# Typed message rows of 26 of 49 node blocks made during the in-degree count

## The chip, the cores and the metric

One core of a Trainium2 chip runs one program. The metric is the device time of one execution in microseconds (us), lower is better. Engines are named as in the profile: PE (TensorE, matrix products and transposes), PEld (its weight loads), DVE (VectorE), ACT (ScalarE), POOL (GpSimd) and SP (SyncE, which only issues DMAs). SPq is the instruction stream of SP.

## The reference, cut to what matters

Four graph layers run over 6250 nodes and 206250 edges, each followed by a residual and a layer norm. The change touches only the first layer. With `W_e` (3 edge types) and `W_n` (3 node types) it computes

```
src = node_feature[edge_src]
parts = [relu(node_feature)]
for t in range(3):
    msg = where(edge_type == t, relu(src @ W_e[t].T + b_e[t]), 0)
    parts.append(segment_sum(msg, edge_dst))
agg = concatenate(parts, axis=1)
updated = where(node_type == t, agg @ W_n[t].T + b_n[t], ...)
```

The kernel multiplies before it sums: for each node and each of the 9 pairs (edge type, node type) it makes one row of 128 numbers, `relu(x W_e[t]) W_n[k]`. Edges gather these **typed rows** later by source, edge type and target's type. So the table of typed rows, `typed_msgs` (49 blocks of 128 nodes, 1152 float32 numbers each, 576 KB per block), must be complete in memory before the gathers begin.

## The kernel before, in words

The program is a sequence of blocks; all engines meet at the end of each. Three of them matter here.

**First block (to about 240 us).** SP loads the edge arrays and then issues, on its one DMA queue and in this order: small paddings (L399 to L403), the copy of all edge features from the input to an internal table (L404, 51.6 MB), seven stores that blank `marks` (L409), and a tail store of `edge_pairs` (L410), and waits for the paddings. Meanwhile the in-degrees are counted. The count has `HB` = 101 steps. In each, DVE makes two sets of one-hot columns (`hist_hot`, L358 and L359) in one of two buffers, and PE adds 16 products of them to a sum (`hist_sum`, L366). `hist_hot` of step n waits until PE has finished step n-2 (`s_hist_mm`), `hist_sum` until its own columns are there (`s_hist_hot`). PE has its steps in a loop of `TB` = 4. After the count, DVE works out edge places and makes the fields of each edge, with small products of PE in between. ACT has nothing to do in this block after it has moved the transposed weights at about 31 us.

**Second block.** SP stores the edge fields; DVE works on a bias.

**Third block, the slot tables (about 266 to 626 us).** 44 steps of a second count (`outs(0, AHEAD)`), and then `GB` = 62 steps n, each of which makes one table of slots: DVE and ACT pick columns, PE transposes them (L1212), ACT and DVE store the result, SP sends it out (`slot_tabs`, L1001), and a share of the other 57 steps of the second count is done. Beside each of the first 49 steps the typed rows of a block pass through the engines, one stage per step: `turn` (PE, L1186, transposes the block of `X` into `ps[2]`), `turned` (ACT, L1150), `message` (PE, L1192, three products into `ps[3]`; ACT, L1156, three relus), `rows` (PE, L1199, three products 384 wide into `ps[4]`, `ps[6]`, `ps[7]`; ACT, L1163 and L1164, copies them to `zrows[b % 2]`), and SP stores `zrows` to `typed_msgs` (L990). Each stage has its semaphore: `s_xT`, `s_xTe`, `s_m`, `s_me`, `s_z`, `s_ze`. There are `MZ` = 2 buffers `zrows`, so the copies of block b wait until the store of block b-2 has landed (`s_mst`). PE's `rows(b)` waits for `s_ze` of block b-1, since it writes the same banks. At step 12 SP loads `marks` back, at step 20 DVE fills them forward, and at step 23 SP stores `edge_pairs`.

The queues and the order within each engine are written out by hand; nothing is planned or reordered by a scheduler.

Of the kernel before, what the change touches and what calls it, by code (L numbers as in the profile page):

```python
# [24 lines left out]
P = 128  # L25
N, E, D, T, FE = 6250, 206250, 128, 3, 64
NB = -(-N // P)
# [120 lines left out]
def build(nc, x, src, dst, attr, etype, weight, ntype, w_e, b_e, w_n, b_n, w1, b1, w3, w3e, b3, out):  # L148
    ctx = ExitStack()
    with ctx:  # L150
# [224 lines left out]
        def along_t(v, n):  # L375
            return v.rearrange("p (g t) -> p g t", t=TU).unsqueeze(2).to_broadcast([P, TG, n, TU])

        in_count = ps[5][:, 0:NB]
        out_count = ps[5][:, 64:64 + NB]

        with nc.Block() as block:
            @block.sync
            def _(sp):

                for col, a in ((src_i, src), (dst_i, dst), (typ_i, etype), (w_c, weight)):
                    sp.dma_start(col[:, 0:EC], a[0:MAIN].rearrange("(p c) -> p c", p=P)).then_inc(s_edges, 16)

                sp.dma_start(next_i[:, 0:EC], dst[1:MAIN + 1].rearrange("(p c) -> p c", p=P)).then_inc(s_edges, 16)
                sp.wait_ge(s_filler, 7)

                for col, a in ((dst_i, dst), (src_i, src), (typ_i, etype), (w_c, weight)):
                    sp.dma_start(col[0:EREST, EC:C], a[MAIN:E].rearrange("(p c) -> p c", c=1)).then_inc(s_rest, 16)
                sp.dma_start(next_i[0:EREST - 1, EC:C], dst[MAIN + 1:E].rearrange("(p c) -> p c", c=1)).then_inc(s_rest, 16)
                sp.dma_start(ntype_i[:, 0:NFULL], ntype[0:NFULL * P].rearrange("(b p) -> p b", p=P)).then_inc(s_rest, 16)
                sp.dma_start(ntype_i[0:NREST, NFULL:NB], ntype[NFULL * P:N].rearrange("(p c) -> p c", c=1)).then_inc(s_rest, 16)

                sp.wait_ge(s_fillf, 13)

                sp.dma_start(edge_fields[0:FRONT, :], front).then_inc(s_pads, 16)  # L399
                tail = slice(FRONT + E, FRONT + E + FILL)  # L400
                sp.dma_start(edge_fields[tail, :].rearrange("(p u) r -> p (u r)", u=U), fillf).then_inc(s_pads, 16)
                sp.dma_start(edge_feats[tail, :].rearrange("(p u) r -> p (u r)", u=U), fille).then_inc(s_pads, 16)
                sp.dma_start(by_place[E:BROWS, :], fillf[0:BROWS - E, 0:NF]).then_inc(s_pads, 16)  # L403
                sp.dma_start(edge_feats[FRONT:FRONT + E, :], attr).then_inc(s_feats, 16)  # L404
                spots = marks.rearrange("(p c) o -> p (c o)", p=P)
                width = MARKS // P
                for c0 in range(0, width, U * FE):
                    c1 = min(c0 + U * FE, width)
                    sp.dma_start(spots[:, c0:c1], fille[:, 0:c1 - c0]).then_inc(s_pads, 16)  # L409
                sp.dma_start(edge_pairs[FRONT + MARKS:EROWS, :].rearrange("(p c) r -> p (c r)", p=TAILP), tail_pairs).then_inc(s_pads, 16)  # L410
                sp.wait_ge(s_pads, 16 * (5 + -(-width // (U * FE))))


# [25 lines left out]
            def _(act):  # L439
# [19 lines left out]
                act.wait_ge(s_wT, T + T * (T + 1) + 2)  # L459
                act.copy(w3ew[:, :], ps[6][0:FE, 0:D]).then_inc(s_wTe, 1)  # L460
                act.wait_ge(s_x, 32)

            @block.tensor
            def _(pe):
# [12 lines left out]
                pe.wait_ge(s_wTe, T + 4)  # L477


                def ins(i, more=TB):  # L480
                    for j in range(more):
                        hist_sum(pe, in_count, i * TB + j, j % 2, opens=isinstance(i, int) and i + j == 0,
                                 closes=isinstance(i, int) and i * TB + j == HB - 1)
                in_steps(pe, PAIRS, ins)
                ins(PAIRS, DST_REST)

                pe.wait_ge(s_tot, 1)
                pe.matmul(ps[2][:, 0:NB], before[:, :], indeg, start=True, stop=True).then_inc(s_pref, 1)
                pe.matmul(ps[2][:, 64:64 + NB], ones[:, :], indeg, start=True, stop=True).then_inc(s_pref, 1)
                pe.wait_ge(s_end, 1)  # L490
                pe.transpose(ps[4][0:NB, 0:P], ends, ident).then_inc(s_endT, 1)
                pe.transpose(ps[4][0:NB, P:2 * P], steps_, ident).then_inc(s_endT, 1)
                pe.wait_ge(s_past, 1)
# [480 lines left out]
        with nc.Block() as block:  # L974
            @block.sync
            def _(sp):
# [7 lines left out]
                sp.dma_start(same_row[:, 0:CHUNKS].rearrange("o (p j) -> (o p) j", j=JB), same[0:CP, :]).then_inc(s_same_st, 16)  # L984
                sp.dma_start(same_row[:, CHUNKS:OVR], zeros[0:1, :]).then_inc(s_same_st, 16)
                for n in range(GB):
                    if 3 <= n < NB + 3:
                        b = n - 3
                        sp.wait_ge(s_ze, 2 * b + 2)
                        sp.dma_start(typed_msgs[b * P:(b + 1) * P, :], zrows[b % MZ]).then_inc(s_mst[b % MZ], 16)  # L990
                    if n == MARK_LOAD:
# [139 lines left out]
            @block.scalar  # L1131
            def _(act):
                def pick(n):
                    k = n % 2
                    here = slots_of(n)
                    slots_here(act, n)
                    at_least(act, s_slot_T, n - 1)
                    act.copy(sl_st[:, k * SLOTS:(k + 1) * SLOTS], here[:, :, SLOC])
                    act.copy(w_st[:, k * SLOTS:(k + 1) * SLOTS], here[:, :, WGT]).then_inc(s_slw_st, 1)

                def store(n):
                    k = n % 2
                    act.wait_ge(s_slot_T, n + 1)
                    at_least(act, s_slot_st[k], 16 * (n // 2))
                    act.copy(tabs[:, k, 0:3, :], ps[k][:, 0:3 * SLOTS].rearrange("p (r g) -> p r g", r=3)).then_inc(s_slot_e, 1)

                def turned(b):
                    act.wait_ge(s_xT, b + 1)
                    at_least(act, s_m, b - 1)
                    act.copy(xTs[b % 2], ps[2][:, 0:P]).then_inc(s_xTe, 1)  # L1150

                def message(b):
                    act.wait_ge(s_m, b + 1)
                    at_least(act, s_z, b - 1)
                    for t in range(T):
                        made = act.activation(mTs[b % 2][:, t * P:(t + 1) * P], ps[3][:, t * P:(t + 1) * P], ACT.Relu,  # L1156
                                              bias=beT[:, t:t + 1])
                    made.then_inc(s_me, 1)

                def rows(b):  # L1160
                    act.wait_ge(s_z, b + 1)
                    at_least(act, s_mst[b % MZ], 16 * (b // MZ))
                    act.copy(zrows[b % MZ][:, 0:T * D], ps[4][:, 0:T * D]).then_inc(s_ze, 1)  # L1163
                    act.copy(zrows[b % MZ][:, T * D:KINDS * D].rearrange("p (k c) -> p k c", k=2),  # L1164
                             psum[:, 6 * 512:8 * 512].rearrange("p (k c) -> p k c", k=2)[:, :, 0:T * D]).then_inc(s_ze, 1)

                for n in range(GB + 1):
                    if n < GB:
                        pick(n)
                    if n >= 1:  # L1170
                        store(n - 1)
                        if n - 1 < NB:
                            turned(n - 1)
                    if 2 <= n < NB + 2:
                        message(n - 2)
                    if 3 <= n < NB + 3:
                        rows(n - 3)

            @block.tensor
            def _(pe):  # L1180
                def outs(j0, j1):
                    for j in range(j0, j1):
                        hist_sum(pe, out_count, HB + j, (HB + j) % 2, opens=j == 0, closes=j == HB - 1)
                def turn(b):
                    at_least(pe, s_xTe, b)
                    pe.transpose(ps[2][:, 0:P], X[:, b * D:(b + 1) * D], ident).then_inc(s_xT, 1)  # L1186

                def message(b):
                    pe.wait_ge(s_xTe, b + 1)
                    at_least(pe, s_me, b)  # L1190
                    for t in range(T):
                        made = pe.matmul(ps[3][:, t * P:(t + 1) * P], weT[:, t * D:(t + 1) * D], xTs[b % 2], start=True, stop=True)  # L1192
                    made.then_inc(s_m, 1)

                def rows(b):
                    pe.wait_ge(s_me, b + 1)
                    at_least(pe, s_ze, 2 * b)
                    for t, to in enumerate((ps[4], ps[6], ps[7])):
                        made = pe.matmul(to[:, 0:T * D], mTs[b % 2][:, t * P:(t + 1) * P], wnT[:, (t + 1) * T * D:(t + 2) * T * D],  # L1199
                                         start=True, stop=True)  # L1200
                    made.then_inc(s_z, 1)

                outs(0, AHEAD)
                for n in range(GB):
                    k = n % 2
                    if n < NB:
                        turn(n)
                    pe.wait_ge(s_sb_st, n + 1)
                    pe.wait_ge(s_slw_st, n + 1)
                    at_least(pe, s_slot_w, n - 1)  # L1210
                    for r, st in enumerate((sl_st, sb_st, w_st)):
                        last = pe.transpose(ps[k][:, r * SLOTS:(r + 1) * SLOTS], st[:, k * SLOTS:(k + 1) * SLOTS], ident)  # L1212
                    last.then_inc(s_slot_T, 1)
                    if 1 <= n < NB + 1:
                        message(n - 1)
                    if 2 <= n < NB + 2:
                        rows(n - 2)
                    outs(*shares[n])


# [1098 lines left out]
```

## Time and profile before

| what | us |
|---|---|
| median of 3 runs | 5259.34 |
| lowest, highest run | 5254.54, 5260.63 |
| the profiled execution | 5261.47 |
| its span | 5259.7 |

The span is the time in which engines work; 1.8 us lie around it. The page's shares of busy time are means over the whole span, and say little about one block: PE is busy for 72% of the span, DVE for 62%, ACT for 23%. The change is read from the first 630 us. A row of a view of instructions gives the start, the duration of a group of neighbours (x16 is sixteen of them) and, in brackets, how long the engine had been idle and what ended that.

### The profile page before, as it was taken

Reading aid. Unit: us, or ns where it says so; the run is one execution under the profiler, and the core shown is the slowest. Engines: PE = TensorE matmul, PEld = TensorE weight load, DVE = VectorE, ACT = ScalarE, POOL = GpSimd, SP = SyncE. Lnnn points to the kernel's source line nnn. Section 1 sums busy time; section 2 is a strip of 40 time slices with the busy share of each in tenths; the row PEclk is TensorE's granted clock in tenths of the full one; section 3 lists DMA queues with packets and bytes.
Section 4 is the critical chain, followed back from the end, with each engine's and each line's share of the span. In section 5 each row is a group of like instructions: output and inputs, shape, how many; then the busy total and the mean of one; then the engine's idle time right before and its main releaser. Section 6 shows DMA issues by size and latency. Waiting matters only on the chain. (4 is left out here: it accounts for less than half of the span.)

```text
span 5259.7 us, 100150 instructions
## 1 busy us (share of the span) xinstructions
PE 3770.5 (72%) x38930; PEld 2751.6 (52%) x38930; DVE 3260.5 (62%) x4529; ACT 1204.4 (23%) x2110; POOL 2254.5 (43%) x2050
## 2 busy tenths in 40 slices
PE   4357755555555555377777676389999599989997
PEld 3345555555555555366666666345555244444444
DVE  7796898999999999455555554756666600230012
ACT  0025655555555555100000000400000200010000
POOL 0051378777777777577777777000000003000300
PEclk9998898999999999688998988699999799989998
DMA  9646797999999999865666656198888267656654
GB/s 315 212 115 238 236 343 276 327 346 340 336 338 340 343 344 330 222 165 166 171 165 165 169 162 158 22 332 305 301 305 304 91 203 227 198 165 202 217 187 142
DMA packets 695303, 1252.28 MB, mean 238 GB/s; under 512 B 366488, under 2 KB 511532, under 8 KB 685772
## 3 DMA queue, kind: packets, MB, share of 16 engines
q1 hardware_dynamic: 564028, 779.03, 46.1%
q10 hardware_dynamic: 60300, 314.88, 15.4%
q0 software_dynamic: 70576, 152.66, 11.4%
q8 instruction: 298, 4.88, 0.4%
q14 instruction: 101, 0.83, 0.0%
HBM read 792.49 MB, written 506.62 MB: 247 GB/s over the span
## 5 line engine op out<-in xcount | busy, mean ns | idle before, releaser
L1398 POOL DMA_INDIRECT big<-typed_msgs,big x988 | 1198.1, 1213 | 376.9 <-issue 307.8
L1446 PE MATMUL psum<-big 128*128 128x98 bf16 x7936 | 859.4, 208 | 649.8 <-DVE big L1428 629.4
L1446 PEld LDWEIGHTS psum<-big 128*128 128x128 bf16 x7936 | 766.0, 97 | 694.1 <-DVE big L1428 673.6
L2088 PE MATMUL psum<-big 128*128 128x512 bf16 (+1 forms) x4704 | 992.1, 373 | 82.6 <-DMA big<-adj 82.6
L1673 PE MATMUL psum<-big 128*128 128x192 f32 x3648 | 743.1, 364 | 307.8 <-DMA big<-typed_msgs,big 302.9
L1581 POOL DMA_INDIRECT big<-typed_msgs,big x836 | 830.8, 994 | 275.3 <-issue 244.8
L1673 PEld LDWEIGHTS psum<-big 128*128 128x128 f32 x3648 | 686.9, 215 | 371.8 <-issue 248.5
L1447 PE MATMUL psum<-big 128*128 128x49 bf16 x7936 | 845.5, 190 | 0.9 <-issue 0.9
L1448 PE MATMUL psum<-big 128*128 128x49 bf16 x7936 | 842.4, 186 | 2.7 <-issue 2.7
L1448 PEld LDWEIGHTS psum<-big 128*128 128x128 bf16 x7936 | 791.7, 100 | 3.1 <-issue 3.1
L2088 PEld LDWEIGHTS psum<-big 128*128 128x128 bf16 x4704 | 460.4, 98 | 605.9 <-DMA big<-adj 83.0
L1447 PEld LDWEIGHTS psum<-big 128*128 128x128 bf16 x7936 | 770.5, 97 | 11.1 <-issue 10.9
L1898 PE MATMUL psum<-big 128*128 128x416 f32 x1984 | 656.1, 494 | 63.4 <-DVE big L1932 62.4
L2135 POOL DMA_INDIRECT big<-spill,spill_row x98 | 92.7, 946 | 1420.0 <-DMA spill<-big 1390.7
L1428 DVE TENSOR_TENSOR big<-big 128x2400 bf16<-128x2400 bf16 x496 | 692.7, 1397 | 0.0
L1595 DVE SCALAR_TENSOR_TENSOR big<-iota,node,big 128x512 f32<-128x512 f32 x456 | 342.0, 750 | 517.4 <-PE psum L1673 502.5
L1425 DVE TENSOR_TENSOR big<-big 128x2048 bf16<-128x2048 bf16 x496 | 602.2, 1214 | 0.0
L1932 DVE STREAM_TRANSPOSE big<-big 128x3136 f32<-128x3136 f32 x124 | 427.2, 3445 | 239.6 <-PE psum L1898 221.2
L1486 ACT CAST big<-psum 128x784 bf16<-128x784 f32 x496 | 404.9, 816 | 675.7 <-PE psum L1448 574.7
L1898 PEld LDWEIGHTS psum<-big 128*128 128x128 f32 x1984 | 378.0, 191 | 341.1 <-issue 82.5
L1488 ACT COPY big<-psum 128x784 f32<-128x784 f32 x496 | 433.3, 874 | 0.0
L1423 DVE TENSOR_TENSOR big<-big 128x800 bf16<-128x800 bf16 x496 | 280.6, 566 | 68.9 <-POOLq L1402 50.1
(320 smaller groups left out, 2732.9 us busy)
## 6 DMA issues: line engine op xcount, KB each, us to landing
wadj<-big ACTq DMA_DIRECT2D x248, 784.0 KB
big<-wadj SPq DMA_DIRECT2D x124, 1568.0 KB, 7.3
big<-adj SPq DMA_DIRECT2D x210, 896.0 KB, 4.8
adj<-big ACTq DMA_DIRECT2D x62, 1568.0 KB
big<-staged SPq DMA_DIRECT2D x247, 384.0 KB, 3.3
staged<-big SPq DMA_DIRECT2D x61, 1536.0 KB
big<-edge_feats SPq DMA_DIRECT2D x456, 128.0 KB, 3.0
edge_feats<-in_edge_attr SPq DMA_DIRECT2D x1, 51562.5 KB, 163.3
```

The source lines that it names most:

```text
L1398: pool.indirect_dma_start(out=sgot4[:, c, u, 0:D], out_offset=None, in_=typed_rows, in_offset=bass.IndirectOffsetOnAxis(ap=pairs4i[:, g, u ...
L1425: dve.tensor_tensor(lo_b[:, q, :, :].rearrange("p t (c d) -> p t c d", d=2), in_twos(lo_ramp).to_broadcast([P, TT, P // 2, 2]), all_column ...
L1428: dve.tensor_tensor(hi_b[:, q, :, 1:4, :].rearrange("p t s (c d) -> p t s c d", d=2), hi.unsqueeze(2).to_broadcast([P, TT, 3, HC // 2, 2]) ...
L1446: pe.matmul(to[:, 0:2 * NB], lo, hi_b[:, q, t, 0:2, 0:NB], start=True, stop=False)
L1447: pe.matmul(to[:, NB:2 * NB], lo, hi_b[:, q, t, 2, 0:NB], start=False, stop=False)
L1448: last = pe.matmul(to[:, NB:2 * NB], lo, hi_b[:, q, t, 3, 0:NB], start=False, stop=True)
L1488: act.copy(wadj_st[:, k, b // 2, :, b % 2 * TT:(b % 2 + 1) * TT], made_in(b % 2)[:, :, NB:2 * NB].rearrange("p t s -> p s t")).then_inc(s_ ...
L1581: pool.indirect_dma_start(out=got4[:, h, u, 0:D], out_offset=None, in_=typed_rows, in_offset=bass.IndirectOffsetOnAxis(ap=pairs4i[:, g, u, ...
L1673: last = pe.matmul(ps[h][:, 0:ACCW], hot4[:, k, u, :], got4[:, pos % QG, u, :], start=(u == 0), stop=(u == U - 1))
L1898: last = pe.matmul(ps[c][:, 0:(b1 - b0) * 32], rows, turned[:, n % RT, q * QROW + b0 * 32:q * QROW + b1 * 32], start=(m == 0), stop=(m == ...
L1932: dve.transpose(turned[:, n % RT, :].rearrange("p (h i) -> p h i", i=32), wring[:, n % RW, :].rearrange("p (h g) -> p h g", g=32)).then_in ...
L2088: last = pe.matmul(ps[c % 2][:, 0:len(blocks) * P], terms_[:, k, b * D:(b + 1) * D], ring_a[:, m % RA, 0:len(blocks), s * P:(s + 1) * P], ...
```

## The change

`EARLY` = 26. The helpers of the typed rows move out of the third block, and are used in two places.

In the first block SP gets the stores of blocks 0 to 25 behind all that it issued before, ACT gets their work behind its last copy of weights, and PE's loop is written out, with the stages of a block between the steps of the count:

```
 # SP, behind L410
+for b in range(EARLY):
+    sp.wait_ge(s_ze, 2 * b + 2)
+    sp.dma_start(typed_msgs[b * P:(b + 1) * P, :], zrows[b % MZ]).then_inc(s_mst[b % MZ], 16)
 # ACT, behind wait_ge(s_x, 32)
+for j in range(EARLY + 2):
+    if j < EARLY:
+        turned(act, j, 0)
+    if 1 <= j < EARLY + 1:
+        relus(act, j - 1, 0)
+    if j >= 2:
+        rows_out(act, j - 2)
 # PE
-in_steps(pe, PAIRS, ins)
-ins(PAIRS, DST_REST)
+pe.wait_ge(s_x, 32)
+done = 0
+for n in range(HB):
+    hist_sum(pe, in_count, n, n % 2, opens=n == 0, closes=n == HB - 1)
+    while done < (n + 1) * (EARLY + 2) // HB:
+        if done < EARLY:
+            turn_x(pe, done, 0)
+        if 1 <= done < EARLY + 1:
+            messages(pe, done - 1, 0)
+        if done >= 2:
+            typed_out(pe, done - 2)
+        done += 1
 ...
 pe.wait_ge(s_end, 1)
+pe.wait_ge(s_ze, 2 * EARLY)
```

The new functions are the old ones; the two waits that matter are these:

```
+def rows_out(act, b):
+    act.wait_ge(s_z, b + 1)
+    at_least(act, s_mst[b % MZ], 16 * (b // MZ))
+    act.copy(zrows[b % MZ][:, 0:T * D], ps[4][:, 0:T * D]).then_inc(s_ze, 1)
 ...
+def typed_out(pe, b):
+    pe.wait_ge(s_me, b + 1)
+    at_least(pe, s_ze, 2 * b)
```

In the third block the 23 remaining blocks 26 to 48 take the places of the first 23 of the 49, so that its steps from n = 26 on have no typed work:

```
 for n in range(GB):
-    if 3 <= n < NB + 3:
-        b = n - 3
+    b = EARLY + n - 3
+    if EARLY <= b < NB:
         sp.wait_ge(s_ze, 2 * b + 2)
```

and likewise on ACT and PE, with b = EARLY + n in place of n.

## Rows read from the trace of the kernel before

**Rows 1.** Windows: stretch, its length, busy us of each engine, clock, DMA share, GB/s
```profile
34.35:159.25 124.90, 69.29 (x1164) 58.94 (x1165) 124.80 (x151) 0.00 (x0) 0.00 (x0) 1.00 1.00 332
...
506.49:591.20 84.71, 83.13 (x666) 63.38 (x665) 66.95 (x151) 69.05 (x193) 20.56 (x23) 1.00 0.95 329
594.84:624.30 29.46, 16.54 (x175) 11.65 (x172) 27.66 (x67) 10.06 (x26) 5.92 (x6) 0.55 0.57 185
```
**Rows 2.** Groups by line, 40.86 to 203.72 us: busy us, mean ns, idle before, releaser
```profile
L358 DVE TENSOR_TENSOR big<-ramp,big 128x2048 bf16<-128x2048 bf16 x101 | 122.8, 1216 | 0.0
L366 PE MATMUL psum<-big 128*128 128x49 bf16 x1600 | 95.5, 229 | 77.1 <-DVE big L359 77.1
```
**Rows 3.** Instructions in order of time, the count's start, DVE's 25th step, its end
```profile
40.86 1.23 DVE L358 TENSOR_TENSOR big<-ramp,big 128x2048 bf16<-128x2048 bf16 x1
...
42.70 0.94 PE L366 MATMUL psum<-big 128*128 128x49 bf16 x16 [12.05 <-DVE big L359]
...
45.70 1.22 DVE L358 TENSOR_TENSOR big<-ramp,big 128x2048 bf16<-128x2048 bf16 x1
...
79.56 1.22 DVE L358 TENSOR_TENSOR big<-ramp,big 128x2048 bf16<-128x2048 bf16 x1
...
203.72 1.68 DVE L585 CAST big<-big 128x1612 f32<-128x1612 int32 x1
...
225.88 0.21 DVE L605 COPY degs<-psum 128x49 f32<-128x49 f32 x1 [0.15 <-DVE small L601]
```
**Rows 4.** Issues of SP in the first block, in order of time
```profile
34.35 0.68 SPq L404 DMA_DIRECT2D edge_feats<-in_edge_attr  x1
35.08 124.13 SPq L409 DMA_DIRECT2D marks<-big  x7
159.25 17.83 SPq L410 DMA_DIRECT2D edge_pairs<-big  x1
```
**Rows 5.** DMA issues of the page: KB each, median us from issue to landing
```profile
edge_feats<-in_edge_attr SPq DMA_DIRECT2D x1, 51562.5 KB, 163.3
```
**Rows 6.** Waits of SP, 0 to 240 us
```profile
SPq L381 <- DMA edge_pairs<-big: 23.5, 1, 23.5
```
**Rows 7.** The tile typed_msgs: its stores' issue, and all its DMAs' landing
```profile
L990 SPq DMA_DIRECT2D typed_msgs<-big x49: 319/326/3624, 367.4 to 592.7; - x49
...
DMA to landing us min/median/max: 2.8/4.9/24.7
```
**Rows 8.** PE in order of time, one step with typed work, clock at 1.00
```profile
499.90 0.31 PE L1186 MATMUL psum<-wide_ident,X 128*128 128x128 f32 x1
500.04 0.49 PE L1212 MATMUL psum<-wide_ident,big 128*128 128x128 f32 x3
500.37 0.83 PE L1192 MATMUL psum<-big,weT 128*128 128x128 f32 x6
501.04 2.10 PE L1199 MATMUL psum<-wnT,big 128*128 128x384 f32 x6
...
506.83 0.96 PE L366 MATMUL psum<-big 128*128 128x49 bf16 x16
507.61 0.31 PE L1186 MATMUL psum<-wide_ident,X 128*128 128x128 f32 x1
```
**Rows 9.** The same, after a gap of 17 us in PE's work
```profile
493.12 0.48 PE L1186 MATMUL psum<-wide_ident,X 128*128 128x128 f32 x1 [17.13 <-ACT big L1150]
493.39 0.85 PE L1212 MATMUL psum<-wide_ident,big 128*128 128x128 f32 x3
494.03 1.59 PE L1192 MATMUL psum<-big,weT 128*128 128x128 f32 x6
495.42 3.87 PE L1199 MATMUL psum<-wnT,big 128*128 128x384 f32 x6
499.12 0.95 PE L366 MATMUL psum<-big 128*128 128x49 bf16 x16
```
**Rows 10.** Windows, as rows 1: a gap in the slot tables
```profile
480.00:495.00 15.00, 1.88 (x9) 1.75 (x10) 1.96 (x6) 2.58 (x8) 0.00 (x0) 0.50 0.27 108
```
**Rows 11.** ACT's copies of typed rows, in order of time
```profile
545.24 0.48 ACT L1163 COPY big<-psum 128x384 f32<-128x384 f32 x1 [0.38 <-PE psum L1199]
545.61 0.81 ACT L1164 COPY big<-psum 128x768 f32<-128x768 f32 x1
```

More of the change, by code:

```diff
@@ L376, in along_t, with turned, relus, turn_x @@
             return v.rearrange("p (g t) -> p g t", t=TU).unsqueeze(2).to_broadcast([P, TG, n, TU])
+        EARLY = 26
+        def turned(act, b, b0):
+            act.wait_ge(s_xT, b + 1)
+            if b >= b0 + 2:
+                act.wait_ge(s_m, b - 1)
+            act.copy(xTs[b % 2], ps[2][:, 0:P]).then_inc(s_xTe, 1)
+        def relus(act, b, b0):
+            act.wait_ge(s_m, b + 1)
+            if b >= b0 + 2:
+                act.wait_ge(s_z, b - 1)
+            for t in range(T):
+                made = act.activation(mTs[b % 2][:, t * P:(t + 1) * P], ps[3][:, t * P:(t + 1) * P], ACT.Relu,
+                                      bias=beT[:, t:t + 1])
+            made.then_inc(s_me, 1)
+        def rows_out(act, b):
+            act.wait_ge(s_z, b + 1)
+            at_least(act, s_mst[b % MZ], 16 * (b // MZ))
+            act.copy(zrows[b % MZ][:, 0:T * D], ps[4][:, 0:T * D]).then_inc(s_ze, 1)
+            act.copy(zrows[b % MZ][:, T * D:KINDS * D].rearrange("p (k c) -> p k c", k=2),
+                     psum[:, 6 * 512:8 * 512].rearrange("p (k c) -> p k c", k=2)[:, :, 0:T * D]).then_inc(s_ze, 1)
+        def turn_x(pe, b, b0):
+            if b > b0:
+                pe.wait_ge(s_xTe, b)
+            pe.transpose(ps[2][:, 0:P], X[:, b * D:(b + 1) * D], ident).then_inc(s_xT, 1)
+        def messages(pe, b, b0):
+            pe.wait_ge(s_xTe, b + 1)
+            if b > b0:
+                pe.wait_ge(s_me, b)
+            for t in range(T):
+                made = pe.matmul(ps[3][:, t * P:(t + 1) * P], weT[:, t * D:(t + 1) * D], xTs[b % 2], start=True, stop=True)
+            made.then_inc(s_m, 1)
+        def typed_out(pe, b):
+            pe.wait_ge(s_me, b + 1)
+            at_least(pe, s_ze, 2 * b)
+            for t, to in enumerate((ps[4], ps[6], ps[7])):
+                made = pe.matmul(to[:, 0:T * D], mTs[b % 2][:, t * P:(t + 1) * P], wnT[:, (t + 1) * T * D:(t + 2) * T * D],
+                                 start=True, stop=True)
+            made.then_inc(s_z, 1)
         in_count = ps[5][:, 0:NB]
@@ L477, in _ @@
                 pe.wait_ge(s_wTe, T + 4)
[L480 to L483, printed above, removed]
-                in_steps(pe, PAIRS, ins)
-                ins(PAIRS, DST_REST)
+                pe.wait_ge(s_x, 32)
[10 more added lines that the diff above has]
+                        done += 1
                 pe.wait_ge(s_tot, 1)
@@ L1145, in store @@
                     act.copy(tabs[:, k, 0:3, :], ps[k][:, 0:3 * SLOTS].rearrange("p (r g) -> p r g", r=3)).then_inc(s_slot_e, 1)
[L1147 to L1165, printed above, removed]
                 for n in range(GB + 1):
@@ L1171, in _ @@
                         store(n - 1)
[L1172 to L1177, printed above, removed]
+                    b = EARLY + n
+                    if EARLY <= b - 1 < NB:
+                        turned(act, b - 1, EARLY)
+                    if EARLY <= b - 2 < NB:
+                        relus(act, b - 2, EARLY)
+                    if EARLY <= b - 3 < NB:
+                        rows_out(act, b - 3)
             @block.tensor
@@ L1183, in outs @@
                         hist_sum(pe, out_count, HB + j, (HB + j) % 2, opens=j == 0, closes=j == HB - 1)
[L1184 to L1201, printed above, removed]
                 outs(0, AHEAD)
@@ L1205, in _ @@
                     k = n % 2
-                    if n < NB:
-                        turn(n)
+                    b = EARLY + n
+                    if b < NB:
+                        turn_x(pe, b, EARLY)
                     pe.wait_ge(s_sb_st, n + 1)
@@ L1213, in _ @@
                     last.then_inc(s_slot_T, 1)
[L1214 to L1217, printed above, removed]
+                    if EARLY <= b - 1 < NB:
+                        messages(pe, b - 1, EARLY)
+                    if EARLY <= b - 2 < NB:
+                        typed_out(pe, b - 2)
                     outs(*shares[n])
```

## The prediction

> **What bounds the kernel now.** I read by stages, since the page's shares are means over blocks with different limits. First the windows: in the stretch of the in-degree count DVE is busy for 124.80 of 124.90 us and PE for 69.29, ACT for none, and the DMA engines are full at 332 GB/s; in the steady steps of the slot tables PE is busy for 83.13 of 84.71 us; in the table steps without typed work DVE is, for 27.66 of 29.46, and PE for only 16.54 [rows 1]. So DVE sets the pace of the count, PE that of a table step with typed rows, DVE that of one without. Then the groups of the count: DVE never waits, PE is idle for 77.1 us, always for DVE's columns [rows 2]. That idle time is where the change puts work. Last I read SP's own stream and its waits, because the change hangs 26 stores on it. There the reader is to see something that DVE's rows don't show. SP issues the feature copy at 34.35; its next seven small stores take 124.13 us to issue, and the one behind them 17.83 [rows 4]. The copy lands 163.3 us after its issue, at 197.7 [rows 5], and the last small store at 159.25 + 17.83 + 23.5 = 200.6, although it is tiny [rows 4, 6]. What SP issues behind the copy is held until the copy is through.
>
> **The change, part by part.** Times are those of the profiled execution.
>
> *(a) The stores of blocks 0 and 1.* SP is free for them only at 177.1, and they stand in the same queue behind a store that lands at 200.6 [rows 4, 6]. One of them is 576 KB: at the 332 GB/s of the copy [rows 1] 1.8 us. So the store of block 0 lands at about 200.6 + 1.8 = 202.4; the floor is 200.6 itself, the ceiling 200.6 + 4.9, the median landing of such DMAs [rows 7].
>
> *(b) Who waits for it.* There are two buffers, so ACT's `rows_out(2)` waits for that landing. PE's `typed_out(3)` waits for `rows_out(2)`. PE comes to it in the pass done = 5, which follows the first n with (n + 1) * 28 // 101 = 6, that is n = 21. Behind this wait stand all further `hist_sum`s of PE. DVE can still make columns 22 and 23, but those of step 24 need sum 22. In the kernel before they start at 79.56 [rows 3]. Now: landing 202.4, ACT's two copies 1.2 (545.24 to 546.42) [rows 11], PE's three wide products 2.1 [rows 8], sum 22 0.95: 206.6. The count is held by 206.6 - 79.6 = **127.0 us**. The stalls of the bursts before that vanish in it. Nothing in the program covers it: DVE has work at every moment of the count [rows 1], and all that it does behind it, up to the end of the block, comes later by as much; the other engines wait for DVE there. Bounds: 125 to 131, from the landing's.
>
> *(c) The bursts after that.* Each pass is a transpose, three products and three wide ones. At the high clock that is 0.14 + 0.67 + 1.94 = 2.75 us, by the starts 499.90, 500.04 (the slot's own transposes, left out), 500.37, 501.04 and the end of the wide ones at 502.98 (501.04 + 2.10, less the 0.16 that one group overlaps the next) [rows 8]. Let PE start sum n at S. The burst follows at S + 0.78 (506.83 to 507.61), sum n+1 ends at S + 0.78 + 2.75 + 0.95, and DVE can start columns n+3 0.04 later, at S + 4.52. In the kernel before it starts them at S + 3.00 (42.70 and 45.70) [rows 3, 8]. So a burst costs 1.5 us of DVE's time, though PE has the idle time on average: 77.1 us against 26 * 2.75 = 71.5; the two buffers can't spread it. At the low clock the burst is 0.27 + 1.39 + 3.70 = 5.36 [rows 9], and it costs 4.1. The passes 6 to 26 still hold DVE: 21. The ends are 21 * 1.5 = 32 and 21 * 4.1 = 86. After the long wait PE begins at the low level: a gap of 15 us has a granted clock of 0.50 (1.2 GHz), and the burst behind it runs slowly until about 499.7, six us into its work [rows 9, 10]. Then PE would be busy for 3.6 * 0.95 + 2.75 = 6.2 us of each 7.3; the steady table steps, busy nearly throughout, have 1.00 (2.4 GHz) and those at 56% have 0.55 [rows 1]. I take 2.0 a burst, nearer to the high clock: **42 us**.
>
> The Trainium skill (TensorE: Matmul & The Clock Gate, HAM oscillation) says that short bursts of products with waits between them can fall back to the low clock before each burst. By it the bursts would all be of the slow kind; the row of the gap agrees for a long pause, and no row shows one of 4 us between such bursts. This is the second rival below.
>
> *(d) ACT's work in the count.* It is idle there, and a table step, which holds the same work and that of the slots, takes it 69.05 / 22 = 3.1 us [rows 1], against 7 us from pass to pass; each piece is wanted one pass later. Nothing, and if ACT were late it would add its delay to a burst. The stores behind the hold: one every 7 us, landing in 3 to 5 [rows 7]; nothing.
>
> *(e) PE's loop written out.* The same instructions, more code to fetch, beside full DMA queues until 200 us but inside the hold; the third block's PE code is written out already, and a sum takes as long there, 0.96 us, as in the loop, 0.94 [rows 3, 8]. Nothing; up to 5 us if fetches come late.
>
> *(f) The wait for `s_ze` before PE's two transposes.* The last pass follows the last sum, and DVE works for 22.2 us after the count before it reads it (203.72 to 225.88) [rows 3]. Nothing.
>
> *(g) The slot tables.* 26 steps lose their typed work. A step with it takes 84.71 / 22 = 3.85 us, one without 29.46 / 10 = 2.95 [rows 1]: 26 * 0.90 = **23.4 us** gained. The rows without typed work ran at a clock of 0.55, so a slower PE is in them. Gaps at the load of `marks`, the fill and the store of `edge_pairs` (steps 12, 20, 23) are DMA or DVE and stay. Ends: 0 if the landings of the tables set the step anyway, 30 if the gaps shrink as 15 MB of stores leave this queue. I take what the rows give.
>
> **Sum.** 127.0 + 42 - 23.4 = +145.6, on the profiled 5261.5: 5407. The median of the runs is 2.1 us lower, so I forecast **5405 us**, 2.8% slower. Its own range is 5388 to 5430.
>
> **Rivals.** *Low clock in the bursts.* Same hold, 86 in place of 42: +189.6, 5449 by the median. For it: the clock is low when PE resumes, and each pass is followed by 4 us of thin work. Against: such a PE would be busy for 3.6 * 0.95 + 5.36 = 8.8 of each 9.9 us, and that is what raised it in the rows [rows 1, 9]. Range 5430 to 5480.
>
> *The stores get through.* Their data travel beside the copy and land in a few us. Then no hold; 25 bursts at 2.0 make +50, less 23.4: +27, 5286. Against it: the tiny store that landed at 200.6, and that a table store or typed store behind others took up to 24.7 us to land [rows 6, 7]; and SP comes to them only at 177.1, so this needs SP's issues to be faster too.
> The Trainium skill (DMA: Bandwidth & Descriptors, Queues, rings and completion order) says that data of one queue carry no barrier, so that a later one may finish before an earlier one. By that the stores could overtake the copy's last packets, 1 to 3 us, not the 120; the trace gives no sign of an overtaking.
>
> *The idle time of PE takes it all* (the other side). Place: the count. If the store of block 0 landed before PE reaches pass 5 at about 77 us, and DVE's columns were far enough ahead that 71.5 us of bursts fill the 77.1 us of idle time [rows 2], the count would keep its length and only the 23.4 be left: 5236. It decides only when both hold; the buffer count speaks against the second, rows 4 against the first.
>
> *No gain in the tables.* The landings of the slot tables set the step: +169, 5428.
>
> **How the numbers follow.** The forecast's case 0.66, low clock 0.20, stores get through 0.08, no gain 0.02, PE's idle time takes it all 0.04. The range of 8 in 10 takes the first two and the last but one, less their tails: 5380 to 5465. About 0.2% (10.5 us) is what a measurement can tell from no change. Slower 0.95, same 0.01, faster 0.04.
>
> **What would show it.** In the changed kernel's profile: DVE idle for some 120 us in the count from about 80 us on, released by PE, PE by ACT, ACT by a DMA of typed_msgs; the first store issued at about 197 with SP's issue stream full until then; the count's end at about 373 instead of 203.7; DVE waits of 1.5 (or 4) us behind each later pass with the clock to match; 36 table steps at 2.95. I am wrong if the first typed store is issued, and lands, before 177, if the count has no gap over 20 us, or if the second block begins before 380.

## The result and the profile after

The changed kernel takes 5423.86 us (median of 4 runs, 5419.55 to 5426.19) against 5259.99 (median of 4, 5254.54 to 5265.01): ratio 1.031, 95% interval 1.0294 to 1.0326. It is slower by 164 us; the profiled spans are 5422.8 and 5259.7, 163.1 apart. The forecast was 5405, range 5380 to 5465.

SP's issues in the first block of the changed kernel, in order of time; they answer to [rows 4]:

```profile
34.92 0.68 SPq L455 DMA_DIRECT2D edge_feats<-in_edge_attr  x1
35.64 123.85 SPq L460 DMA_DIRECT2D marks<-big  x7
159.53 18.09 SPq L461 DMA_DIRECT2D edge_pairs<-big  x1
177.66 216.02 SPq L464 DMA_DIRECT2D typed_msgs<-big  x26
```

The waits of all engines up to 420 us (us in total, times, longest):

```profile
DVE big L358 <- PE psum L366: 182.4, 26, 119.4
...
ACT big L401 <- DMA typed_msgs<-big: 121.3, 1, 121.3
PE psum L425 <- ACT big L402: 114.9, 1, 114.9
```

This is the hold, and its order is read from the right: a DMA, ACT, PE, DVE, one wait of each. The instructions at its end, in order of time:

```profile
201.49 0.48 ACT L401 COPY big<-psum 128x384 f32<-128x384 f32 x1 [121.27 <-DMA typed_msgs<-big]
201.87 0.80 ACT L402 COPY big<-psum 128x768 f32<-128x768 f32 x1
...
202.81 4.18 PE L425 MATMUL psum<-wnT,big 128*128 128x384 f32 x6 [114.93 <-ACT big L402]
...
206.79 1.76 PE L366 MATMUL psum<-big 128*128 128x49 bf16 x32
...
207.92 1.22 DVE L358 TENSOR_TENSOR big<-ramp,big 128x2048 bf16<-128x2048 bf16 x1 [119.39 <-PE psum L366]
...
217.45 1.22 DVE L358 TENSOR_TENSOR big<-ramp,big 128x2048 bf16<-128x2048 bf16 x1 [2.99 <-PE psum L366]
...
223.85 1.23 DVE L358 TENSOR_TENSOR big<-ramp,big 128x2048 bf16<-128x2048 bf16 x1 [1.47 <-PE psum L366]
```

DVE's 25th step starts at 207.92, not at 79.56 [rows 3]. The two rows of DVE after it are the waits for the first two bursts behind the hold. Three bursts of PE, by their wide products: the first, in which the clock rose, the second, at the high clock, and a later one at the low clock throughout:

```profile
213.60 2.89 PE L425 MATMUL psum<-wnT,big 128*128 128x384 f32 x6
...
220.80 2.10 PE L425 MATMUL psum<-wnT,big 128*128 128x384 f32 x6
...
311.01 3.67 PE L425 MATMUL psum<-wnT,big 128*128 128x384 f32 x6
```

The windows, with the columns of [rows 1]: the hold, the rest of the count, the slot tables; then the slot tables of the kernel before:

```profile
80.00:205.00 125.00, 8.95 (x64) 6.31 (x64) 5.39 (x7) 2.36 (x7) 0.00 (x0) 0.51 0.96 324
205.00:389.02 184.02, 151.17 (x1524) 118.21 (x1522) 126.05 (x155) 50.03 (x127) 0.00 (x0) 0.82 0.17 69
546.01:791.07 245.06, 159.41 (x1388) 118.34 (x1387) 187.52 (x425) 114.49 (x316) 55.90 (x52) 0.69 0.65 213
```

```profile
360.73:626.54 265.81, 213.73 (x1726) 162.41 (x1725) 193.16 (x425) 168.10 (x472) 51.49 (x52) 0.88 0.73 254
```

In the hold the DMA engines are full and PE, DVE and ACT nearly idle; behind it the DMA engines are nearly empty (0.17) and PE and DVE wait for each other.

The account, from the two traces: the count starts 0.6 us later (41.42 for 40.86); the hold is 207.92 - 79.56 - 0.6 = 127.8 (DVE's long wait of 119.4, 8.0 us of four waits for bursts before it, and small change); from there to the end of the count, at 389.02, it takes 181.1 us, before 203.72 - 79.56 = 124.2 [rows 3], so 56.9 more; the slot tables take 20.8 less. 0.6 + 127.8 + 56.9 - 20.8 = 164.5; the remaining 1.4 us come back later.

### The profile page after: what moved, and what is told of

It is laid out like the page before. It is cut to its first block and busy times, and to the rows that moved or that the text cites. A ratio compares the mean times of both kernels' runs of the same rounds, so it can differ in the third digit from the quotient of the medians.

```text
span 5422.8 us, 100007 instructions
## 1 busy us (share of the span) xinstructions
PE 3806.8 (70%) x38930; PEld 2770.6 (51%) x38930; DVE 3257.1 (60%) x4529; ACT 1213.1 (22%) x2110; POOL 2251.6 (42%) x2050
## 5 line engine op out<-in xcount | busy, mean ns | idle before, releaser
L358 DVE TENSOR_TENSOR big<-ramp,big 128x2048 bf16<-128x2048 bf16 x202 | 246.4, 1220 | 189.5 <-PE psum L366 189.4
```

## The experiments

All are edits of the changed kernel; the code shown for e4, e6 and e9 is against e2, e1 and e5. Ratios are to the kernel before on the same chip.

**e2: no stores in the count.** The 26 stores come from X (wrong contents) behind the last sum; ACT's `rows_out` waits for no landing of the first 26 blocks.

```
-for b in range(EARLY):
-    sp.wait_ge(s_ze, 2 * b + 2)
-    sp.dma_start(typed_msgs[b * P:(b + 1) * P, :], zrows[b % MZ]).then_inc(s_mst[b % MZ], 16)
 sp.wait_ge(s_pads, ...)
+sp.wait_ge(s_hist_mm, HB)
+for b in range(EARLY):
+    sp.dma_start(typed_msgs[b * P:(b + 1) * P, :], X[:, 0:KINDS * D]).then_inc(s_pads, 16)
```

> The changed kernel without SP's 26 stores in the count, so that nothing there waits for a landing; in their place 26 stores of the same size, from X (wrong contents), are issued behind the last sum of the count, and nothing in the block waits for them. Theory (the landing of the first store holds the count for 128 us, and 25 bursts cost 2.6 us each): the hold goes, 5260 + 65 - 21 = 5304 us, up to 5312 if the late stores delay the edge fields. Rival (PE and ACT can't keep up with the work in the count, whatever the stores do): the long wait stays, 5424. Second rival (most bursts cost nothing without the low clock of the long pause): 5275.

Measured: 5315.84, ratio 1.0099 (1.0073 to 1.0125). The long wait is gone; PE and ACT do all of the work without it. What is left is the bursts' cost, in DVE's waits up to 400 us:

```profile
DVE big L358 <- PE psum L366: 75.4, 26, 3.8
```

That is 2.9 us for each of 26; I had 2.6. The longest is near the 4.1 that the prediction works out for a burst at the low clock. The count takes 41.96 to 282.51, 240.6 us, 77.7 more than before.

**e3: the tables alone.** Blocks 0 to 25 are not made at all (their stores as in e2), PE's count has no typed work.

> The kernel before in the count (PE's steps written out, no typed work), and the changed one in the slot tables: blocks 0 to 25 are not made at all; as in e2, 26 stores from X are issued behind the count to keep the bytes. This prices the gain in the tables alone. Theory: 26 steps at 0.8 to 0.9 us, 5260 - 21 = 5239 us. Rival (the landing of the tables sets the step and the changed kernel's shorter tables come from something else): 5260.

Measured: 5242.38, ratio 0.9962 (0.9948 to 0.9976), 20 us faster. Its slot tables take from 363.51 to 608.31, 244.8 us, against 265.8. Its count, without typed work, takes 41.70 to 204.45, as long as before. So the gain is the tables', and no kernel below gains clearly more. Its window of the count:

```profile
42.00:203.00 161.00, 94.84 (x1584) 80.66 (x1584) 161.00 (x201) 0.00 (x0) 0.00 (x0) 0.50 0.98 322
```

The thin products alone leave PE at the low clock (0.50).

**e4: as e2, with PE's work spread.** A pass is cut into 4 pieces, laid over the steps of the count.

```
-while done < (n + 1) * (EARLY + 2) // HB:
+while done < (n + 1) * 4 * (EARLY + 2) // HB:
+    k, piece = done // 4, done % 4
+    if piece == 0 and k < EARLY:
+        turn_x(pe, k, 0)
+    if piece == 0 and 1 <= k < EARLY + 1:
+        messages(pe, k - 1, 0)
+    if piece >= 1 and k >= 2:
+        typed_out(pe, k - 2, piece - 1)   # one wide product
+    done += 1
```

> As e2, but PE's typed work is spread: a pass of a block is cut into 4 pieces (transpose with the three small products, and each of the three wide products alone), and 112 pieces are laid over the 101 steps of the count. PE does the same work. Theory (a burst of 2.75 us or more is longer than two buffers of columns can bridge; 0.7 us is not): the count keeps its length to within 10 us, 5239 to 5250. Rival (the sum of PE's work, or its clock, lengthens the count, wherever the work stands): as e2, 5304 or more.

Measured: 5241.01, ratio 0.9956 (0.9939 to 0.9973). The same products as e2, 75 us fewer. The same wait, and the window of the count:

```profile
DVE big L358 <- PE psum L366: 2.7, 8, 1.3
```

```profile
42.00:203.00 161.00, 155.59 (x1879) 121.99 (x1880) 157.97 (x195) 55.86 (x152) 0.00 (x0) 0.94 0.98 322
```

PE is busy for 155.59 of 161 us and DVE for 157.97: the idle time of PE [rows 2] does take nearly all of the 26 blocks, as the rival on the other side said, if the pieces are short. The count takes 41.64 to 208.62, 167.0 us, 4.1 more than before.

**e8: the spread alone,** in the changed kernel with its stores.

> The changed kernel with PE's work spread as in e4 and nothing else: the hold alone. Theory (the two costs are independent): the hold stays at 129 us, the 57 us of the bursts go: 5260 + 129 - 21 = 5368 us. Rival (the bursts are slow mostly because of the low clock after the hold, and the spread pieces suffer as much): 5400 or more.

Measured: 5368.37, ratio 1.0211 (1.0195 to 1.0227). The two costs add, and each goes by itself: 5368.37 and the 56.9 us of the bursts make 5425, and the changed kernel takes 5423.86. DVE's waits:

```profile
DVE big L358 <- PE psum L366: 133.2, 11, 129.0
```

**e1: the copy on ACT's queue.**

```
-sp.dma_start(edge_feats[FRONT:FRONT + E, :], attr).then_inc(s_feats, 16)
 act.dma_start(X3[0:NREST, NFULL, :], x[NFULL * P:N, :]).then_inc(s_x, 16)
+act.dma_start(edge_feats[FRONT:FRONT + E, :], attr).then_inc(s_feats, 16)
```

> The changed kernel, with the copy of the edge features issued by ACT on its own queue, behind its load of X, and not by SP; all else is as it was. Theory (the typed stores stand behind the copy in SP's queue): the single hold of 120 us goes. The stores then share the 16 DMA engines with a copy of 60 KB packets; at one such packet of 2.9 us ahead of each of a store's 8 pieces a store lands after some 23 us, two buffers give a block per 12 us until the copy is through, and I expect about 5345 us; if the stores pass more freely, down to 5300. Rival (the DMA engines are full, so a store waits for the copy's end from whichever queue it comes): one hold to about 200 us as before, 5424.

Measured: 5475.44, ratio 1.0403 (1.0385 to 1.042), slower than every case I had. The copy now starts at 27.6, before SP's last small load is through, the node types of the last 106 nodes, 4 bytes each. It landed only when the copy was done (27.6 + 166.9 = 194.5), and DVE went on with it at 194.8. The wait, and the DMA queues from 40 to 85 us (packets, MB, share of 16 engines; q10 is ACT's, q1 is SP's):

```profile
DVE big L641 <- DMA ntype_i<-in_node_type: 192.8, 1, 192.8
```

```profile
q10 hardware_dynamic: 244, 14.64, 100.1%
q1 hardware_dynamic: 39, 0.00, 0.0%
```

**e6: the same, behind the loads.** ACT waits for `s_rest` before it issues the copy.

```
+act.wait_ge(s_rest, 16 * 7)
 act.dma_start(edge_feats[FRONT:FRONT + E, :], attr).then_inc(s_feats, 16)
```

> As e1, but ACT waits for the last loads of SP (the node types, 6250 pieces of 4 bytes) before it issues the copy on its own queue. Theory (in e1 those small pieces went beside the copy at 2.4 per us and DMA engine, and held the start of the count until 194 us; behind the loads the same rate gives the stores' 8 pieces in 3.4 us): the count starts at about 41 us and has no hold of 100 us, about 5310 us. Rival 1 (a store's pieces take turns one by one with packets of 2.9 us, 23 us a store): 5345 to 5380. Rival 2 (a store waits for the end of the copy from any queue): 5424.

Measured: 5423.97, ratio 1.0319 (1.0302 to 1.0335), by the number the second rival. But the queues tell another mechanism. Packets, MB and share of SP's queue (q1) and ACT's (q10), from 60 to 100 us and from 100 to 190:

```profile
q10 hardware_dynamic: 216, 12.96, 98.6%
q1 hardware_dynamic: 217, 0.19, 1.3%
...
q10 hardware_dynamic: 489, 29.34, 99.2%
q1 hardware_dynamic: 488, 0.38, 1.2%
```

SP's packets do travel beside the copy, one for one: each small piece waits for one packet of 60 KB. Ahead of the first typed store stand the paddings. The seven stores for `marks` alone are some 8 pieces each on every DMA engine; at 2.9 us a piece, 56 of them use up the copy's whole time. The first typed store, issued at 66.70, landed after 137.5 us; up to 190 us none of SP's packets reached 2 KB, and a typed row has 4.6, so that store's own pieces had not begun. So it is the first rival's mechanism with a larger number of pieces in it than I had counted. My expectation of 5310 failed on the rate of 2.4 pieces per us that I read out of e1: in its trace SP's queue moved 3777 pieces from 28 to 32 us, while ACT's moved 1.1 MB, about one packet of 60 KB for each DMA engine, and 112 pieces from 40 to 185, beside the full copy. (The Trainium skill, DMA: Bandwidth & Descriptors, Queues, rings and completion order, says that a DMA engine takes turns between queues by packets that typically hold some 9 to 17 descriptors. By this trace a turn was one row of some 1 KB (0.19 MB in 217) against one of 60 KB, 217 to 216, and that is what is reckoned with here.)

**e7 and e5: the copy cut up.** 55 pieces of 3750 edges in SP's own queue, 7 where the copy stood, 1 or 2 behind each typed store, the rest last. The waits for the copy count all 55. e7 has PE's bursts, e5 the spread work of e4.

```
-sp.dma_start(edge_feats[FRONT:FRONT + E, :], attr).then_inc(s_feats, 16)
+send(7)
 ...
     sp.dma_start(typed_msgs[b * P:(b + 1) * P, :], zrows[b % MZ]).then_inc(s_mst[b % MZ], 16)
+    send(2 if b % 3 == 2 else 1)
+send(E // UNIT - sent[0])
```

> The cut copy of e5 with PE's work in bursts as in the changed kernel: what the hold alone is worth in a correct kernel. Theory: the bursts stay at 2.6 to 2.9 us each, the hold goes: 5315 us as e2, up to 5325 for the later end of the copy. Rival: bursts and landings meet, 5340 or more.

> A version that should keep the gain and lose both costs: the changed kernel with PE's work spread as in e4, its 26 stores at their old place in SP's order, and the copy of the edge features cut into 55 equal pieces (3750 edges each), of which 7 go out where the copy stood, 1 or 2 behind each typed store, and the rest last. Theory (a store waits only for what was issued before it in its queue): a store has at most 2 pieces of 2.9 us ahead of it and lands within two passes of 5.8 us, the count keeps its length; the bytes of the stores push the end of the copy to about 245 us, where the second block waits for it: 5241 as e4, plus 0 to 15: 5247 us. Rival (full DMA engines keep a store from landing in time, whatever its queue holds): each block waits 10 us or more, above 5300.

Measured: e7 5327.15, ratio 1.013 (1.0114 to 1.0145); e5 5253.58, ratio 0.9993 (0.9984 to 1.0002). The order in SP's queue alone takes the hold away (e7 is 97 us below e6 on the same chip: the count takes 239.0 us for 349.8, and 17 us go to a later end of the copy, by SP's wait for the edge fields, 34.8 us for 17.6). It lies 2 us above the range that I gave. e5 nearly keeps the count (167.5 us, 4.6 more than before), but has no gain that its interval shows; I had expected 5247. SP's wait in its second block shows where it went, first in e5, then in the changed kernel:

```profile
SPq L861 <- DMA edge_fields<-big: 32.6, 1, 32.6
```

```profile
SPq L845 <- DMA edge_fields<-big: 17.6, 1, 17.6
```

The 15 MB of stores push the copy's end, and behind it in the same queue stand the edge fields: 15 us later. With the 4.6 of the count that is nearly all of what the tables give.

**e9: the end of the copy held back.** The last 6 pieces go behind the stores of the edge fields, and the wait for the copy to the end of the third block.

```
-send(E // UNIT - sent[0])
+send(E // UNIT - sent[0] - 6)
 ...
     sp.dma_start(edge_fields[FRONT + MAIN:FRONT + E, :], F3[0:EREST, EC, :]).then_inc(s_fields, 16)
+for r0 in range(E - 6 * UNIT, E, UNIT):
+    sp.dma_start(edge_feats[FRONT + r0:FRONT + r0 + UNIT, :], attr[r0:r0 + UNIT, :]).then_inc(s_feats, 16)
-sp.wait_ge(s_feats, 16 * 55)
```

> As e5, but the last 6 of the 55 pieces of the copy are issued behind the stores of the edge fields in the second block, and the wait for the copy moves from the second block to the end of the third (for unsorted edges it stays where it was). In e5 SP waited 32.6 us for the edge fields to land, against 17.6 in the kernel before. Theory (the typed stores' bytes pushed the copy's end onto that wait): the 15 us go, 5239 us, as the two kernels without typed stores in the count. Rival (e5's lack of a gain comes from its count or its tables): 5253.

e9 and e10 ran on a chip on which the kernel before takes 5816.36 us, so only ratios carry over. Measured: 5800.21, ratio 0.9972 (0.9958 to 0.9987): faster than the kernel before, by 16 us there; the changed kernel was not run on that chip, its ratio elsewhere is 1.031. 0.9960 was expected and lies in the interval. The count takes 41.18 to 208.38, 167.2 us, against 162.9. That is no more than in e4 (167.0), whose ratio is 0.9956, so the count does not explain why e9 gains less than e4; the difference is within the two intervals. SP's waits for the fields:

```profile
SPq L867 <- DMA edge_fields<-big: 8.3, 1, 8.3
```

**e10: two pieces a pass,** else as e9.

> As e9, with a pass of a block cut into 2 pieces of some 1.4 us and not 4 (transpose, small products and the first wide one; the two other wide ones). Theory (a piece costs DVE its length less 1.2 us, what the two buffers bridge): 0.2 us for the longer piece, 5 us in all: 5239 to 5246. Rival (any piece longer than PE's 0.66 us of idle time in a step costs the surplus, 0.7 us and more for each of 52): 5275.

Measured: 5812.07, ratio 0.9996 (0.9983 to 1.0009), 12 us more than e9. DVE's waits are near the theory:

```profile
DVE big L358 <- PE psum L366: 7.8, 20, 1.2
```

They grew by 5 us from e9's 2.9, as expected; the count as a whole by 7 (174.2 us), and 5 us of the 12 I can't place: the runs of either kernel lie up to 33 us apart, and the two profiled ones (5795.26, and 5799.28 of e9) stand the other way round. The interval also leaves out what I had expected, 5239 to 5246 of 5260 or 0.9960 to 0.9973. The theory has the waits right and the total not. The rival of 0.7 us a piece (5275 of 5260, 1.0029) is excluded.

## Why the prediction was right, step by step

*(a), (b) the hold.* Right in place, order and size: 127.8 against 127.0. Some of that closeness is luck: the store landed at about 201.4, 1 us earlier than I had, and PE's wide products took 4.2 us, not 2.1. I had priced them at the high clock, though PE had been idle for 115 us and [rows 9] have 3.87 behind a gap. The first store was issued from 177.66 on, as in (a); the 197 among my signs contradicts (a) and was wrong. e2, e7 and e8 show that it is the landing, in this queue, and nothing in PE or ACT; e6 shows that another queue for the copy does not free it. The case "the stores get through" is refuted.

*(c) the bursts.* The mechanism was right, and the term too small: 56.9 against 42. DVE's 21 waits behind the hold are 182.4 - 8.0 - 119.4 = 55.0 us, 2.6 each (8.0 us are the four before it). PE waited for nothing but DVE in this stretch, so ACT has no part in it. Of the remaining 2 us DVE's own operations, 1221 and 560 ns for 1216 and 558, are 0.5; for the rest, two neighbouring operations overlap by 0.08 us (209.06 + 0.56 against 209.54), and at each wait that is lost.

Of the 21 bursts 7 ran at the high clock throughout and cost 1.45 to 1.48 us, as worked out; 4 ran at the low clock throughout and cost 3.72 to 3.74, not 4.1, since a burst there takes 5.0 us (309.48 to 314.52) and not 5.36. In the other ten, 2.72 to 3.15, the level changed inside the burst. The clock was 0.82 on average behind the hold, so neither of my two cases was pure; by 1.5 and 4.1 a mean of 2.6 is as 4 bursts in 10 at the low clock. I had taken 1 in 5, a choice between two values that no row gave. The "low clock" rival was a third of the way right. (The Trainium skill's account of a clock that falls back between bursts, TensorE: Matmul & The Clock Gate, HAM oscillation, was nearer than I gave it credit for: the granted clock in the trace goes back and forth, where the steady table steps have 1.00 [rows 1].)

One figure of [rows 1] misleads here: the 1.00 beside the count of the kernel before, with PE busy for 69.29 of 124.90 us, is no measurement. That trace has no clock record before 373 us, and its first transposes of the tables, at 357.21 and 359.28, still take 0.46 and 0.48 us, those from 366.20 on 0.31 as in [rows 8]. e3 has clock records from 34 us on and shows 0.50 for the same count. A sum of 16 thin products takes 0.95 to 0.96 us at either level [rows 8, 9], so the count's own length does not tell. So the thin products alone keep PE at the low level, and the typed ones raise it: e4 has 0.59 from 20 to 60 us and 1.00 from 60 to 200.

e4 shows that this cost isn't PE's total work: with the pieces spread the granted clock is 0.94, and the waits are 2.7 us. It takes away the length of the bursts and the low clock at once; how the two share the cost is read from the bursts above.

*(d), (e), (f).* Nothing, as said. ACT's waits in the rest of the count are for PE. The written-out loop costs nothing in the count (that of e3 has no typed work and lasts 162.75 us, before 162.86, and starts 0.8 us later).

*(g) the tables.* 20.8 against 23.4. The steps without typed work take 108.65 us for 36, 3.0 each and not 2.95; e3 gives 20 to 21 by itself.

The sum: +145.6 forecast, +163.1 measured in the profiled runs, near the upper end of the forecast's own case (5388 to 5430); of the 17.5 us 14.9 are the bursts (13 by longer waits, 2 by the lost overlap), 2.6 the tables, and the hold's 0.8 and the start's 0.6 are given back later. So the term that was too small is (c); the count ended at 389.02, where I had said about 373.

## What to carry to other kernels

Before work with stores is moved beside a long transfer, read the queue and not only the idle engines: a DMA behind a 160 us copy lands after it, and with two buffers the third block of results stops everyone who waits. A second queue is no way out when its small pieces take turns with 60 KB packets; cutting the long copy and ordering its pieces by hand is. And idle time in short gaps, 0.66 us a step here, is filled by pieces that the buffers can bridge, not by bursts of the same sum: 26 blocks of typed rows lengthened the count by 78 us in bursts of 2.75 us and more (e2) and by 4 us in pieces of some 0.7 (e4).

## What was unexpected of the hardware

Two queues on the same DMA engines alternated one packet for one, as unequal as these were: 216 packets of 60 KB beside 217 of less than 2 KB in 40 us (e6). 106 pieces of 4 bytes so took until 194.8 us (e1), the whole of the copy. At 2.9 us a turn 50 turns fit on one DMA engine in the 145 us from 40 to 185, and SP's queue moved 112 packets there: they would stand on two or three of the engines, which is an estimate and was not looked at.
